# A wait of POOL in the middle of each group's eight gathers, in both layers of a two-layer graph network

## The chip, the cores and the metric

The kernel runs on one core of a Trainium2 chip. The metric is the device time of one execution in microseconds; the median of several runs is compared. Beside the timed runs there is one execution recorded by the hardware profiler, from which all rows here come.

## The reference, cut to what matters

There are 12,500 nodes with 128 features and 200,000 edges sorted by destination, `dst`, with random sources, `src`. Layer 0 is an attention layer over the edges, layer 1 sums the neighbours with edge features and puts two matrix products behind them. Both read one row of a node table for each edge, by `src`.

```python
# layer 0: loops added to the edges
xl = (x @ W_l).reshape(N, HEADS, C); xr = (x @ W_r).reshape(N, HEADS, C)
h = xl[src] + xr[dst]
e = jnp.einsum('ehc,hc->eh', leaky_relu(h, 0.2), att)
p = jnp.exp(e - segment_max(e, dst)[dst])
alpha = p / segment_sum(p, dst)[dst]
out = segment_sum(alpha[:, :, None] * xl[src], dst).reshape(N, HID) + bias + x
x = layernorm(x + layernorm(out) * gamma + beta)
# layer 1
neigh = segment_sum(x[src] + edge_attr_128, dst)
h = leaky_relu((2.0 * x + neigh) @ W1 + b1, 0.01)
x = layernorm(x + (h @ W2 + b2))
```

## The kernel before, in words

The work has three phases with a barrier of all engines behind the first and the second. In the first, `node_loop` makes the tables `xl_table` (528 bytes a node: the product and four linear terms) and `xr_table` from `x`. The second is layer 0, the third layer 1.

Both layers walk over 196 groups of 1024 edges (128 partitions, `T` = 8 edges each). Four sets of buffers (`U` = 4) go around: `src_idx`, `rows`, `dst_row` and others. Each engine has its own program, a loop over groups, and the engines meet by semaphores.

SP loads for each group the indices `src_idx` (4 KB, line 614 in layer 0, line 1416 in layer 1) and the larger pieces: in layer 0 the destinations of the group repeated on all partitions (`dst_row`, 513 KB, line 607) and a window of `xr_table`; in layer 1 the edge features (`dst_row` again, 512 KB, line 1419) and a window of `x1_table`. In layer 0 the indices of a group are loaded one group ahead (`AHEAD` = 1), in layer 1 three groups behind the group whose sum is done (`BACK` = 3).

POOL issues the gathers: for each group eight indirect DMAs of 128 rows each (line 671 from `xl_table`, line 1446 from `x1_table`), each with one index per partition. In layer 0 it waits for the indices and for the set of rows (`rows_free0`, signalled by DVE's line 1124 four groups before); in layer 1 for the indices alone, which are loaded only when the set is free. Each gather adds 16 to the set's own semaphore `gathered0` or `gathered1` when its data has landed.

PE waits for the whole group, 128 on that semaphore, before its first product of the rows (`sources`, line 694, and `sum_group`, line 1460). In layer 0 a step of PE is: `sources` of the next group, two transposes, `targets` (line 703), `sum_up` of the last group (line 745), `attend` (line 729), `pick_last` (line 767). ACT and DVE make the softmax between them; DVE's line 1112 waits for `attend`, ACT's line 925 for `sum_up`. In layer 1 PE sums features and rows into a bank and signals `neigh_summed`; DVE's line 1631 adds the bank to the nodes' sums, and PE's lines 1483 to 1496 make the two products of one window of nodes, a window a group.

`wait_alone` is a wait for a semaphore as an instruction of its own, followed by one that adds 1 to a count of waits.

Of the kernel before, what the change touches and what calls it, by code (L numbers as in the profile page):

```python
# [30 lines left out]
T = 8  # L31
# [116 lines left out]
def wait_alone(eng, waits, sem, value):  # L148


    eng.wait_ge(sem, value)
    eng.sem_inc(waits, 1)
# [20 lines left out]
def build(nc, a, out, edges, groups, blocks):  # L173
# [6 lines left out]
    with ctx:  # L180
# [81 lines left out]
        def by_head(t):  # L262
# [15 lines left out]
        pool_waits, pe_waits, v_waits, sp_waits, act_waits = (  # L278
            nc.alloc_semaphore(n) for n in ("pool_waits", "pe_waits", "v_waits", "sp_waits", "act_waits"))
        sems = {}  # L280

        def S(name):
            if name not in sems:
                sems[name] = nc.alloc_semaphore(name)
            return sems[name]
# [45 lines left out]
        with nc.Block() as block:  # L331
            @block.sync
            def _(sp):
                for t, n in ((w_lr[:, 0:D], "W_l"), (w_lr[:, DW:DW + D], "W_r")):
                    sp.dma_start(t, a[n]).then_inc(S("products_in"), 16)

                def load(q):
                    if q.at_least(2 * R):
                        sp.wait_ge(S("x_taken"), q.times(1, 1 - 2 * R))
                    s = q.c % (2 * R)  # L340
                    sp.dma_start(ring_x[s], x_pair[q.times(1)]).then_inc(S(f"x_in{s}"), 16)

                def store(q):
                    s = q.c % R
                    sp.wait_ge(S("xl_ready"), q.times(1, 1))
                    sp.dma_start(xl_pair[q.times(1)], ring_w[s]).then_inc(S(f"xl_out{s}"), 16)
                    sp.wait_ge(S("xr_ready"), q.times(1, 1))
                    sp.dma_start(xr_pairs[q.times(1)], xr_pair[:, q.times(1)]).then_inc(S("xr_out"), 16)

                node_loop(sp, pairs, [(load, 0), (store, 7)])  # L350
                for g in range(AHEAD):
                    sp.dma_start(src_idx[g][:, :], bass.AP(a["src"].tensor, g * G, [[T, P], [1, T]]))\
                      .then_inc(S(f"src_in0{g}"), 16)
                sp.wait_ge(S("xr_out"), 16 * pairs)
                for s in range(R):
                    sp.wait_ge(S(f"xl_out{s}"), 16 * (pairs // R))
# [260 lines left out]
        with nc.Block() as block:  # L617
# [45 lines left out]
            @block.gpsimd  # L663
            def _(pool):
                with pool.Fori(0, groups // U) as j:
                    for s in range(U):

                        wait_alone(pool, pool_waits, S(f"src_in0{s}"), j * 16 + 16)
                        wait_alone(pool, pool_waits, S(f"rows_free0{s}"), j + 1)
                        for t in range(T):  # L670
                            pool.indirect_dma_start(rows[s][:, t, :], None, xl_table[:, :],  # L671
                                                    bass.IndirectOffsetOnAxis(ap=src_idx[s][:, t:t + 1], axis=0))\
                                .then_inc(S(f"gathered0{s}"), 16)
# [729 lines left out]
        with nc.Block() as block:  # L1403
# [35 lines left out]
            @block.gpsimd  # L1439
            def _(pool):  # L1440
                with pool.Fori(0, groups // U) as j:
                    for s in range(U):

                        wait_alone(pool, pool_waits, S(f"src_in1{s}"), j * 16 + 16)
                        for t in range(T):
                            pool.indirect_dma_start(rows[s][:, t, 0:D], None, x1_table[:, :],  # L1446
                                                    bass.IndirectOffsetOnAxis(ap=src_idx[s][:, t:t + 1], axis=0))\
                                .then_inc(S(f"gathered1{s}"), 16)
# [284 lines left out]
```

## Time and profile before

| | us |
|---|---|
| median of 3 runs | 4110.53 |
| lowest and highest | 4109.94 and 4111.07 |
| profiled execution, span of its instructions | 5652.3 |
| of this busy: PE, POOL, DVE, ACT | 3416.6, 2973.6, 2121.7, 1585.3 |

The page gives no time for the profiled execution but its span; what lies around the first and the last instruction is not in it. The profiled execution is far longer than the timed ones. In rows of the timeline the columns are the start in us, the duration in us, engine, line, operation, what it writes and reads, how many instructions the row merges, and in brackets the idle time of the engine before it and what ended it. An engine name with a q behind it is its queue, where DMAs are issued.

### The profile page before, as it was taken

How to read it: one execution, taken by the hardware profiler on the slowest of the kernel's cores; microseconds unless marked ns; L12 is line 12 of the kernel's file. 1: busy time of each engine (PE TensorE's matmuls, PEld its weight loads, DVE VectorE, ACT ScalarE, POOL GpSimd, SP SyncE). 2: the span in 40 equal slices, each digit the busy share in tenths (PEclk: the TensorE clock that was granted, in tenths of full speed). 3: DMA queues.
4: the chain of work that ended last, by engine and by line, in shares of the span. 5: the costliest groups of instructions: out<-in, count | busy, mean ns of one | idle time of the engine just before them, and what ended most of it. 6: DMA issues, size and time to landing. Idle time of an engine off the chain costs nothing. (4 is left out here: it accounts for less than half of the span.)

```text
span 5652.3 us, 80469 instructions
## 1 busy us (share of the span) xinstructions
PE 3416.6 (60%) x19294; PEld 2795.9 (49%) x19295; DVE 2121.7 (38%) x8176; ACT 1585.3 (28%) x3447; POOL 2973.6 (53%) x3194
## 2 busy tenths in 40 slices
PE   5667676766666766767666455545555555555554
PEld 4455454545445544545544444445455455545454
DVE  4454554545544544545545122222222222222222
ACT  3343443334333433334333111111111111111111
POOL 2454454544554554555552656555555565555554
PEclk8787888778887878778877677777777777777777
DMA  7333333333333333333332533333333333333332
GB/s 227 81 97 89 91 94 86 93 82 92 92 88 86 94 87 86 90 85 95 91 88 59 102 91 93 92 90 93 92 92 93 92 93 92 93 91 93 92 93 70
DMA packets 459582, 525.88 MB, mean 93 GB/s; under 512 B 199115, under 2 KB 359287, under 8 KB 459551
## 3 DMA queue, kind: packets, MB, share of 16 engines
q1 hardware_dynamic: 266498, 268.35, 16.3%
q0 software_dynamic: 100352, 208.93, 15.3%
q10 hardware_dynamic: 92701, 48.23, 3.0%
q8 instruction: 13, 0.21, 0.0%
q14 instruction: 18, 0.15, 0.0%
HBM read 471.23 MB, written 53.95 MB: 93 GB/s over the span
## 5 line engine op out<-in xcount | busy, mean ns | idle before, releaser
L671 POOL DMA_INDIRECT rows<-xl_table,src_idx x1568 | 1482.2, 945 | 1458.0 <-DVE wmsg L1124 655.5
L1446 POOL DMA_INDIRECT rows<-x_table,src_idx x1568 | 1480.4, 944 | 1102.7 <-issue 605.8
L1491 PE MATMUL ph<-ident,relu_h 128*128 128x128 f32 x196 | 83.9, 428 | 1103.0 <-DVE relu_h L1636 726.0
L1491 PEld LDWEIGHTS ph<-ident,relu_h 128*128 128x128 f32 x196 | 33.0, 168 | 1164.0 <-DVE relu_h L1636 755.5
L703 PE MATMUL ph<-node_of,xr_win 128*128 128x512 f32 x784 | 517.8, 797 | 5.9 <-issue 5.1
L745 PE MATMUL pA<-wmsg,edge_of 128*128 128x136 f32 x3136 | 430.7, 293 | 94.9 <-issue 56.9
L911 ACT ACTIVATE relu_h<-ph 128x512 f32<-128x512 f32 x392 | 232.1, 597 | 849.3 <-PE ph L703 551.9
L1532 ACT ACTIVATE relu_h<-ph,b 128x128 f32<-128x128 f32 x196 | 72.0, 367 | 1383.6 <-PE ph L1496 1044.1
L745 PEld LDWEIGHTS pA<-wmsg,edge_of 128*128 128x128 f32 x3136 | 402.7, 199 | 104.8 <-issue 100.5
L767 PE MATMUL pA<-win,last_node 128*1 128x136 f32 x392 | 99.0, 345 | 573.7 <-ACT win L925 513.1
L729 PE MATMUL pT<-att_heads,relu_h 128*128 128x48 f32 x3136 | 383.6, 272 | 79.0 <-issue 52.5
L729 PEld LDWEIGHTS pT<-att_heads,relu_h 128*128 128x128 f32 x3136 | 375.6, 194 | 71.7 <-issue 39.4
L965 ACT ACTIVATE node_of<-dst_row,first_node 128x1024 f32<-128x1024 int32 x196 | 406.3, 2073 | 5.6 <-issue 4.9
L694 PE MATMUL ph<-ident,rows 128*128 128x128 f32 x1568 | 309.2, 362 | 57.8 <-issue 57.8
L1112 DVE TENSOR_TENSOR logits<-pT,rows 128x32 f32<-128x32 f32 x196 | 39.8, 203 | 752.8 <-remote 626.2
L767 PEld LDWEIGHTS pA<-win,last_node 128*1 128x1 f32 x392 | 20.8, 80 | 608.6 <-issue 605.7
L694 PEld LDWEIGHTS ph<-ident,rows 128*128 128x128 f32 x1568 | 253.1, 189 | 122.1 <-issue 117.4
L1460 PE MATMUL pT<-node_of,dst_row 128*128 128x128 f32 x1568 | 300.1, 372 | 0.0
L1460 PEld LDWEIGHTS pT<-node_of,dst_row 128*128 128x128 f32 x1568 | 296.3, 290 | 0.8
L1631 DVE TENSOR_TENSOR xr<-xr,pA 128x128 f32 x98 | 28.3, 288 | 707.9 <-DMA w_lr<-in_W_r 699.1
L703 PEld LDWEIGHTS ph<-node_of,xr_win 128*128 128x128 f32 x784 | 191.8, 271 | 192.3 <-issue 180.7
L1460 PE MATMUL pA<-edge_of,dst_row 128*128 128x128 f32 x1568 | 285.3, 359 | 0.8 <-issue 0.7
(174 smaller groups left out, 6322.4 us busy)
## 6 DMA issues: line engine op xcount, KB each, us to landing
dst_row<-in_dst SPq DMA_DIRECT2D x196, 513.0 KB
dst_row<-in_edge_attr SPq DMA_DIRECT2D x195, 512.0 KB
rows<-xl_table,src_idx POOLq DMA_INDIRECT x1568
rows<-x_table,src_idx POOLq DMA_INDIRECT x1568
sums_table<-win ACTq DMA_DIRECT2D x196, 68.0 KB
xr_win<-xr_table SPq DMA_DIRECT2D x196, 64.0 KB
relu_h<-x_table SPq DMA_DIRECT2D x196, 64.0 KB
out_x<-relu_h ACTq DMA_DIRECT2D x196, 64.0 KB
```

The source lines that it names most:

```text
L671: pool.indirect_dma_start(rows[s][:, t, :], None, xl_table[:, :], bass.IndirectOffsetOnAxis(ap=src_idx[s][:, t:t + 1], axis=0))\
L694: pe.matmul(h[:, t, :], rows[s][:, t, 0:D], ident[:, :], start=(t % 4 == 0), stop=False, is_transpose=True)
L703: return [pe.matmul(h[:, k:k + 4, :], xr_of[:, :], by_tile[:, k:k + 4, :], start=False, stop=stop) for k in range(0, T, 4)]
L729: ins = pe.matmul(out_t[:, t, :], relu_h[0][:, t, :], att_heads[:, :], start=(t == 0), stop=(t == T - 1))
L745: ins = pe.matmul(pA[k][:, 0:WC], edge_of[k][:, t, :], w[:, t, :], start=(t == 0), stop=(t == T - 1))
L767: pe.matmul(pick, last_node[:, g.c % U:g.c % U + 1], win[:, :], start=True, stop=True)\
L911: act.activation(relu_h[0][:, k:k + 4, :], h, ACT.Relu, scale=1.0 - GAT_SLOPE)\
L965: act.activation(in_tiles(node_of[g.c % 2][:, :]), ids, ACT.Abs, scale=-1.0, bias=first_node[:, s:s + 1])\
L1446: pool.indirect_dma_start(rows[s][:, t, 0:D], None, x1_table[:, :], bass.IndirectOffsetOnAxis(ap=src_idx[s][:, t:t + 1], axis=0))\
L1460: ins = pe.matmul(bank, m[:, t, :], one_hot[:, t, :], start=(k == 0 and t == 0), stop=(k == 1 and t == T - 1))
L1491: pe.transpose(across_bank, x1_slot[s], ident[:, :]).then_inc(S("x1_across"), 1)
L1532: act.activation(of, z_bank, ACT.Identity, bias=b1[:, 0:1])
```

## The change

Between the fourth and the fifth gather of each group, in both layers, POOL waits until its semaphore says that the first four gathers of this group have landed (64 above what the earlier rounds of this set left, 128 for each).

```diff
                         wait_alone(pool, pool_waits, S(f"src_in0{s}"), j * 16 + 16)
                         wait_alone(pool, pool_waits, S(f"rows_free0{s}"), j + 1)
                         for t in range(T):
+                            if t == T // 2:
+                                wait_alone(pool, pool_waits, S(f"gathered0{s}"), j * (16 * T) + 16 * (T // 2))
                             pool.indirect_dma_start(rows[s][:, t, :], None, xl_table[:, :],
                                                     bass.IndirectOffsetOnAxis(ap=src_idx[s][:, t:t + 1], axis=0))\
                                 .then_inc(S(f"gathered0{s}"), 16)
...
                         wait_alone(pool, pool_waits, S(f"src_in1{s}"), j * 16 + 16)
                         for t in range(T):
+                            if t == T // 2:
+                                wait_alone(pool, pool_waits, S(f"gathered1{s}"), j * (16 * T) + 16 * (T // 2))
                             pool.indirect_dma_start(rows[s][:, t, 0:D], None, x1_table[:, :],
                                                     bass.IndirectOffsetOnAxis(ap=src_idx[s][:, t:t + 1], axis=0))\
                                 .then_inc(S(f"gathered1{s}"), 16)
```

## Rows read from the trace of the kernel before

**Rows 1.** The page: span, and busy time of each engine.
```profile
span 5652.3 us, 80469 instructions
...
PE 3416.6 (60%) x19294; PEld 2795.9 (49%) x19295; DVE 2121.7 (38%) x8176; ACT 1585.3 (28%) x3447; POOL 2973.6 (53%) x3194
```

**Rows 2.** Table of stretches: layer 0, between, layer 1, end; clock and DMA last.
```profile
104.90:3034.09 2929.19, 1987.22 (x10757) 1458.70 (x10757) 1453.23 (x6061) 1130.60 (x2359) 1482.18 (x1568) 0.80 0.35 92
3034.09:3109.34 75.25, 41.69 (x191) 31.02 (x190) 36.61 (x155) 18.36 (x55) 0.01 (x1) 0.74 0.12 28
3109.34:5617.16 2507.82, 1296.33 (x7899) 1238.21 (x7899) 556.41 (x1728) 381.49 (x862) 1480.37 (x1568) 0.76 0.34 93
5617.16:5652.30 35.14, 19.11 (x137) 18.14 (x137) 9.70 (x37) 6.15 (x18) 0.00 (x0) 0.79 0.06 14
```

**Rows 3.** Timeline of POOL, two groups of layer 0 behind each other, first and last.
```profile
1609.69 0.94 POOL L671 DMA_INDIRECT rows<-xl_table,src_idx  x1 [0.30 <-issue]
1610.94 0.94 POOL L671 DMA_INDIRECT rows<-xl_table,src_idx  x1 [0.30 <-issue]
...
1627.16 0.94 POOL L671 DMA_INDIRECT rows<-xl_table,src_idx  x1 [0.30 <-issue]
```

**Rows 4.** What POOL waited for, whole span: us in total, times, longest.
```profile
POOL rows L671 <- DVE wmsg L1124: 655.5, 61, 16.9
...
POOL rows L1446 <- DMA src_idx<-in_src: 496.8, 109, 6.8
...
POOL rows L671 <- DMA src_idx<-in_src: 319.4, 85, 4.6
```

**Rows 5.** What DVE and ACT waited for in layer 0, whole span.
```profile
DVE logits L1112 <- remote: 626.2, 62, 16.6
```
```profile
ACT win L925 <- remote: 699.7, 129, 16.6
```

**Rows 6.** Timeline of all engines around a standstill in layer 0.
```profile
1617.23 1.89 PE L729 MATMUL pT<-att_heads,relu_h 128*128 128x48 f32 x16
...
1631.05 0.28 ACT L925 ACTIVATE win<-pA 128x136 f32<-128x136 f32 x1 [14.12 <-remote]
1631.14 0.21 DVE L1112 TENSOR_TENSOR logits<-pT,rows 128x32 f32<-128x32 f32 x1 [12.77 <-remote]
...
1631.48 0.61 PE L767 MATMUL pA<-win,last_node 128*1 128x136 f32 x2 [12.37 <-ACT win L925]
```

**Rows 7.** Timeline of DVE behind the last gather of layer 1.
```profile
5628.67 0.29 DVE L1631 TENSOR_TENSOR xr<-xr,pA 128x128 f32 x1 [3.83 <-PE pA L1460]
...
5634.80 0.29 DVE L1631 TENSOR_TENSOR xr<-xr,pT 128x128 f32 x1 [0.17 <-PE pT L1460]
...
5641.02 0.29 DVE L1631 TENSOR_TENSOR xr<-xr,pT 128x128 f32 x1 [2.32 <-PE pT L1460]
```

**Rows 8.** Timeline, layer 1: SP's load of indices and the gather it releases, twice.
```profile
4004.03 0.33 SPq L1416 DMA_DIRECT2D src_idx<-in_src  x1
...
4006.48 0.94 POOL L1446 DMA_INDIRECT rows<-x_table,src_idx  x1 [4.25 <-DMA src_idx<-in_src]
...
4029.51 0.33 SPq L1416 DMA_DIRECT2D src_idx<-in_src  x1
...
4031.82 0.94 POOL L1446 DMA_INDIRECT rows<-x_table,src_idx  x1 [4.63 <-DMA src_idx<-in_src]
```

**Rows 9.** DMA: the gathers' queue, and loads with median us to landing last.
```profile
q0 software_dynamic: 100352, 208.93, 15.3%
...
sums<-xl_table SPq DMA_DIRECT2D x51, 132.0 KB, 2.3
...
sums<-in_x SPq DMA_DIRECT2D x51, 128.0 KB, 2.5
...
rows<-in_x SPq DMA_DIRECT2D x50, 128.0 KB, 2.1
```

**Rows 10.** Timeline: last gather of the first group, first product that reads its rows.
```profile
113.79 0.94 POOL L671 DMA_INDIRECT rows<-xl_table,src_idx  x1 [0.30 <-issue]
...
120.25 1.94 PE L694 MATMUL ph<-ident,rows 128*128 128x128 f32 x8 [9.22 <-issue]
```

## The prediction

> **What bounds the kernel now.** I read the page first, then the table of stretches, then POOL's own rows, and last the places where the whole core stands still.
>
> The page shows no engine that is full: PE is busy 60% of a span of 5652.3 us, POOL 53% [rows 1]. The span itself is the first thing to explain: the runs have a median of 4110.53 us, so the profiled execution is 5652.3 - 4110.5 = 1541.8 us (38%) longer than the runs that are timed. Whatever fills those 1541.8 us is in the profile and not in the time, and a reading of the waits at face value would be a reading of something else.
>
> The stretches split the span at POOL's first and last gather of each layer [rows 2]: 104.9 us of node work ahead, 2929.19 us for layer 0 (196 groups, 14.9 us each), 75.25 us between, 2507.82 us for layer 1 (12.8 us each), 35.14 us at the end. The three parts without gathers come to 104.9 + 75.25 + 35.14 = 215.3 us.
>
> POOL does nothing in the layers but issue gathers, eight to a group, 1568 to a layer. Each is 0.94 us busy with 0.30 us before the next [rows 3]: a start every 1.2475 us or so (1609.69 to 1627.16 is 14 steps, 1.248 each). The reader is to see that this run crosses a border of groups without a wider step: a wait on POOL that is already satisfied costs nothing that shows. So POOL alone needs 8 x 1.248 = 9.98 us for a group, 392 x 9.98 = 3913 us for all, and with the 215.3 us around it 4128 us. The median of the runs is 4110.5, 0.4% below that. I read this as: in the timed runs POOL issues gathers back to back all the time, and its issue rate is what the kernel takes.
>
> The check from the other side: in the profile POOL stands idle beyond its own steps for 2929.2 + 2507.8 - 3913 = 1524 us, and 1541.8 us is what the profiled execution is longer. Nearly all of its waits for freed buffers (655.5 us) and for indices (319.4 and 496.8 us) [rows 4] are then in the profile alone. What makes them is seen in the chain of waits and the timeline. DVE and ACT wait 626.2 and 699.7 us for something the profile calls remote in layer 0 [rows 5]. In one such place PE starts its last product at 1617.23 for 1.89 us, and nothing on ACT, DVE or PE starts until ACT does at 1631.05, DVE at 1631.14, PE at 1631.48 [rows 6]: signals of PE that should be there at 1619.1 act 12 us later. After the last gather the same loop takes 6.2 us a group: DVE's addition starts right behind PE's end at 5628.67, 5634.80 and 5641.02 [rows 7]. The other engines of layer 1 thus need about 6.2 us a group where POOL needs 9.98. In layer 0 PE is busy 1987.22/196 = 10.1 us a group at a granted clock of 0.80, that is between 8.1 us (all at full clock) and 10.1, so close behind POOL.
>
> **The change, part by part.** It removes nothing and moves nothing: per group one wait and one semaphore increment on POOL, between the fourth and the fifth gather, 392 in all. The gathers, their number and their order stay. The increment and a wait that is satisfied show no cost at the borders of groups [rows 3]: I take 0. Queued behind the wait on POOL are the group's gathers five to eight and all later groups' gathers; PE waits for all eight of a group. No DMA of SP or ACT is moved or passed, since they are other queues.
>
> The wait is not satisfied when POOL comes to it. It asks for the landing of a gather that POOL has just issued, so POOL idles from the end of the fourth gather until its rows are in SBUF and the semaphore says so. That gap takes the place of the 0.30 us that stand there now. No row shows a gather awaited by POOL, so I bound the gap.
>
> Nearest rows from below: a 4 KB index load is issued by SP at 4004.03 (0.33 us) and POOL's waiting gather starts at 4006.48; the next pair is 4029.51 and 4031.82 [rows 8]: 2.3 to 2.45 us from the start of the issue to POOL's start. Plain loads of 128 to 132 KB land 2.1 to 2.5 us after issue [rows 9], so for 64 KB the size hardly counts. If these times ran from the start of the gather instruction, whose descriptors are written while it is busy, 2.3 - 0.94 = 1.4 us would be left as the gap; if from its end, 2.3 to 2.5 us. Nearest row from above: the first group's last gather starts at 113.79 and ends at 114.73; PE's first product that reads the rows starts at 120.25 [rows 10], 5.5 us later, while ACT's 6.9 MB of zeros (the page's largest single issue) were being written. That is a landing under load. In the layers DMA is a third busy [rows 2], and the gathers' queue moves a gather's data in 0.153 x 5652.3/3136 = 0.28 us of each engine [rows 9], so a single collision with another transfer adds tenths, not microseconds. I take 2.3 us, nearer to the small loads: the last descriptors of a gather are ready only at its end, which pulls to the upper case, and the early ones are already under way, which pulls to the lower.
>
> The sum: 2.3 - 0.30 = 2.0 us a group, 2.0 x 392 = 784 us. None of it is covered: the cover would be POOL's idle time, and the timed runs have none. Against the profile's own parts that is 4128 + 784 = 4912; against the median, which I use, 4110.5 + 784 = 4895 us. The new period is 12.0 us; PE needs 8.1 to 10.1 in layer 0 and 6.2 in layer 1, so POOL stays the bound. Later starts of later gathers also mean later indices and free buffers, but those are asked for a ring of three or four groups ahead, and POOL being slower makes them earlier by comparison.
>
> The Trainium skill, in "DMA: Bandwidth & Descriptors", section "Anatomy of one DMA — SWDGE (gpsimd) path", gives about 2.0 us plus bytes/436e3 for one such DMA, nearly all of it the confirmation that the data has landed. By it a gather of 64 KB takes 2.15 us as an estimate; laid behind the gather's end that would give (2.15 - 0.30) x 392 = 725 us and 4836 us, laid from its start 357 us and 4468 us. The plain loads of [rows 9] agree with it, and no row here shows a gather's.
>
> **The rivals.**
>
> Absorbed (no change). Taken at face value the profile has POOL idle 1524 us at borders of groups, 3.9 us a group, more than the 2.0 us added; a wait in the middle would only take the place of the one at the border, and the time would stay 4110. For it: those waits are large and real in the profile [rows 4]. Against it: they would have to be in the timed runs too, and 4110.5 has no room for them beside 3913 us of issuing. It decides if the step between gathers is shorter in timed runs.
>
> Partly absorbed. If the 0.30 us between gathers come with profiling, the step is 0.94 us, POOL needs 7.5 us a group and has 2.4 us of slack in the (4110.5 - 215.3)/392 = 9.94 us of a group. Then POOL's period is 8 x 0.94 + 2.3 = 9.8 us, nothing is added, and we are at the case above; halfway, with a step of 1.1 us, it is 8.8 - 0.16 + 2.3 = 10.9 us against 9.94, 392 x 1.0 = 390 us, and 4500 us. Against it: the fit of 4128 to 4110 would be chance.
>
> Longer landing, or a cold PE. With a gap of 3.5 us (a 513 KB row of node numbers or a 512 KB block of edge features in the way every group) it is 3.2 x 392 = 1254 us and 5365 us. A PE that idles 4 us of 12 and falls to the lower clock in layer 0 would need up to 10.1 x 0.80/0.50 = 16.2 us a group there if all of it ran at 1.2 GHz. Against that: in the profile, at 14.9 us a group and so with more idle time, the mean granted was 0.80 and the work 10.1 us [rows 2], under the 12.0 us of the new period. I give it only the same upper end.
>
> Faster. The late signals of PE [rows 6] hold all engines while POOL issues without a pause, and at 1631.05 they come 2.95 us after POOL's last gather ended (1628.1). If a stream of gathers holds them back, a pause in mid-group lets them through, and PE, ACT and DVE run sooner. In the profile that is worth up to 626 us in layer 0. It pays only if those stalls, not POOL, set the timed 9.94 us a group, and if POOL with its pause still needs less: with a step of s that is 7s + 0.94 + 2.3 < 9.94, so s under 0.96 us, where the profile has 1.248 and the busy time alone is 0.944. At 0.944 it would be 9.85 us a group, 392 x 0.09 = 35 us and 4075 us.
>
> **How the numbers follow.** Full price with a gap of 1.9 to 2.9 us (4740 to 5130 us): 0.62. Gap of 1.4 to 1.9, or partly absorbed (4500 to 4740): 0.17. Longer landing or cold PE (5130 to 5400 and beyond): 0.14. Absorbed: 0.05. Faster: 0.02. The predicted time is that of the first, 4895 us. The range must hold 0.8: all of the first, most of the second and half of the third, 4550 to 5250 us. A measurement of this kernel, whose three runs span 0.03%, tells a change from none at about 0.2%; slower by more than that are the first three cases, 0.93, within it 0.05, faster 0.02.
>
> **What the profile of the changed kernel would show.** The fifth gather of each group preceded by idle time of about 2.3 us, ended by a DMA, 392 times, where 0.30 us stand now; the busy time of a gather still 0.94 us and 1.25 us between the others. POOL's waits for freed buffers and indices shrink, since in the profile (not in the time) they are there to be replaced; so the profiled span grows by less than the timed 784 us. If the gap were near 1.4 or 3.5 us, the size is wrong and the step is right. If the gap is 2.3 us and the time still 4110, then the reading of POOL as the bound is wrong, and with it the whole.

## The result, and the profile after

The changed kernel takes 5063.02 us (median of 4 runs, 5053.62 to 5066.17) beside 4110.8 us (4109.94 to 4112.89) for the kernel before: a ratio of 1.2315, 95% interval 1.23 to 1.2329. The forecast was 4895 us, range 4550 to 5250. It is 952 us slower, 2.43 us for each of 392 groups; forecast were 784 us and 2.0 us.

The kernel before has two times: medians of 4110 to 4117 us on some chips (the first kind below) and of 5660 to 5670 us on others (the second kind); every comparison below was made on one chip, and the profile of before [rows 1, 2] is, by its span, of the second kind, that of after of the first.

The page of the changed kernel, the lines that answer to [rows 1], and below them those of its slices for PE's clock:

```profile
span 5061.6 us, 80959 instructions
...
PE 3402.5 (67%) x19294; PEld 2808.9 (55%) x19295; DVE 2115.3 (42%) x8176; ACT 1582.5 (31%) x3447; POOL 2975.7 (59%) x3194
...
PEclk9888888888888888888887777777777777777777
```

The span is within 2 us of the run's own time of 5063.47. The busy times are within 1% of those of before: nothing was added to do. The table of stretches, cut as in [rows 2] at POOL's first and last gather of a layer:

```profile
106.40:2610.10 2503.70, 1904.68 (x10814) 1409.89 (x10812) 1472.04 (x6112) 1136.00 (x2381) 1484.48 (x1568) 0.86 0.42 108
2610.10:2671.60 61.50, 28.84 (x134) 22.29 (x134) 24.74 (x103) 9.83 (x33) 0.12 (x1) 0.75 0.06 17
2671.60:5041.40 2369.80, 1387.60 (x7990) 1318.94 (x7990) 550.04 (x1752) 385.35 (x873) 1479.92 (x1568) 0.78 0.36 98
5041.40:5061.60 20.20, 8.04 (x46) 7.42 (x46) 2.71 (x13) 2.69 (x8) 0.08 (x1) 0.73 0.06 15
```

Layer 0 takes 12.8 us a group, layer 1 12.1 us. What POOL waited for, beside [rows 4]:

```profile
POOL rows L673 <- DMA rows<-xl_table,src_idx: 601.4, 196, 7.3
POOL rows L1450 <- issue: 479.2, 1372, 61.4
POOL rows L1450 <- DMA rows<-x_table,src_idx: 472.1, 196, 5.8
POOL rows L673 <- issue: 429.3, 1372, 11.5
```

The waits for freed rows and for indices are gone. In their place stand 196 waits in each layer for POOL's own gathers: 601.4/196 = 3.07 us in layer 0, 472.1/196 = 2.41 us in layer 1. The other 1372 gathers of each layer have their 0.30 us of "issue" as before. Their sum less the 0.30 us that stood there before is 601.4 + 472.1 - 392 x 0.30 = 956 us, beside the 952 us timed. The timeline of POOL at two pauses, one in each layer; the number in brackets is the idle time:

```profile
1603.04 0.95 POOL L673 DMA_INDIRECT rows<-xl_table,src_idx  x1 [0.30 <-issue]
1604.29 0.94 POOL L673 DMA_INDIRECT rows<-xl_table,src_idx  x1 [0.30 <-issue]
1609.44 0.94 POOL L673 DMA_INDIRECT rows<-xl_table,src_idx  x1 [4.21 <-DMA rows<-xl_table,src_idx]
...
4008.74 0.94 POOL L1450 DMA_INDIRECT rows<-x_table,src_idx  x1 [0.30 <-issue]
4012.06 0.94 POOL L1450 DMA_INDIRECT rows<-x_table,src_idx  x1 [2.38 <-DMA rows<-x_table,src_idx]
```

Layer 1 is regular (2.31 to 2.49 us in a row of nine pauses). Layer 0 goes up and down: of twelve pauses behind each other, seven took 2.33 to 2.44 us and five 3.29 to 4.48 us. SP's queue at the long one above shows a large load close by, the 513 KB of destination numbers, issued while the fourth gather was being made (1604.29 to 1605.23):

```profile
1604.41 0.33 SPq L605 DMA_DIRECT2D dst_near<-in_dst  x1
...
1604.84 0.38 SPq L607 DMA_DIRECT2D dst_row<-in_dst  x1
```

Whether a pause is long goes by the time of that load. In the timelines from 400 to 2400 us there are 156 pauses. In 65 the load was issued before the fourth gather ended, and they took 3.85 us on average (2.82 to 4.58); in 91 it was issued later, and they took 2.43 us (2.30 to 2.83), as in layer 1.

Who waits for the pause is seen from PE: before its first product of a group's rows it now stands 535.0 us in layer 0 and 727.1 us (366.2 + 360.9) in layer 1, each time for a gather.

```profile
PE ph L696 <- DMA rows<-xl_table,src_idx: 535.0, 191, 15.7
PE pT L1464 <- DMA rows<-x_table,src_idx: 366.2, 98, 4.5
PE pA L1464 <- DMA rows<-x_table,src_idx: 360.9, 97, 4.6
```

### The profile page after: what moved, and what is told of

Same layout as the page of the kernel before. It is cut to its first block and busy times, and to the rows that moved or that the text cites. A ratio compares the mean times of both kernels' runs of the same rounds, so it can differ in the third digit from the quotient of the medians.

```text
span 5061.6 us, 80959 instructions
## 1 busy us (share of the span) xinstructions
PE 3402.5 (67%) x19294; PEld 2808.9 (55%) x19295; DVE 2115.3 (42%) x8176; ACT 1582.5 (31%) x3447; POOL 2975.7 (59%) x3194
## 3 DMA queue, kind: packets, MB, share of 16 engines
q1 hardware_dynamic: 266498, 268.35, 17.9%
## 5 line engine op out<-in xcount | busy, mean ns | idle before, releaser
L673 POOL DMA_INDIRECT rows<-xl_table,src_idx x1568 | 1484.6, 947 | 1030.7 <-DMA rows<-xl_table,src_idx 601.4
L696 PE MATMUL ph<-ident,rows 128*128 128x128 f32 x1568 | 299.6, 354 | 535.2 <-DMA rows<-xl_table,src_idx 535.0
L1464 PE MATMUL pT<-node_of,dst_row 128*128 128x128 f32 x1568 | 354.7, 418 | 366.2 <-DMA rows<-x_table,src_idx 366.2
L1464 PE MATMUL pA<-edge_of,dst_row 128*128 128x128 f32 x1568 | 355.2, 419 | 361.4 <-DMA rows<-x_table,src_idx 360.9
L1464 PEld LDWEIGHTS pT<-node_of,dst_row 128*128 128x128 f32 x1568 | 331.0, 321 | 382.0 <-issue 382.0
L1464 PEld LDWEIGHTS pA<-edge_of,dst_row 128*128 128x128 f32 x1568 | 331.8, 322 | 377.3 <-issue 377.3
L705 PE MATMUL ph<-node_of,xr_win 128*128 128x512 f32 x784 | 537.4, 825 | 0.0
L747 PE MATMUL pA<-wmsg,edge_of 128*128 128x136 f32 x3136 | 409.7, 284 | 68.9 <-DVE edge_of L1159 68.7
L747 PEld LDWEIGHTS pA<-wmsg,edge_of 128*128 128x128 f32 x3136 | 381.7, 190 | 77.5 <-issue 73.5
L1159 DVE TENSOR_TENSOR edge_of<-dst_rel,pT 128x1024 f32<-128x1024 f32 x196 | 239.3, 1221 | 96.8 <-DVE dst_rel L1156 91.4
L1635 DVE TENSOR_TENSOR xr<-xr,pT 128x128 f32 x98 | 28.3, 288 | 541.8 <-PE pT L1464 541.8
L1146 DVE COPY carry_f<-carry_f 4x1 f32<-4x1 f32 x196 | 27.7, 142 | 538.7 <-PE pT L812 538.4
```

What stands on the lines that cost most here:

```text
L696: pe.matmul(h[:, t, :], rows[s][:, t, 0:D], ident[:, :], start=(t % 4 == 0), stop=False, is_transpose=True)
L705: return [pe.matmul(h[:, k:k + 4, :], xr_of[:, :], by_tile[:, k:k + 4, :], start=False, stop=stop) for k in range(0, T, 4)]
L747: ins = pe.matmul(pA[k][:, 0:WC], edge_of[k][:, t, :], w[:, t, :], start=(t == 0), stop=(t == T - 1))
L1159: one_hot = lambda k: v.tensor_tensor(edge_of[k][:, :, :], dst_rel[:, :].unsqueeze(2).to_broadcast([P, T, P]), near_row.unsqueeze(1).to_br ...
L1464: ins = pe.matmul(bank, m[:, t, :], one_hot[:, t, :], start=(k == 0 and t == 0), stop=(k == 1 and t == T - 1))
```

## The experiments

**1. A wait that is already satisfied.** In both layers, in the place of the wait of the change (layer 0 is shown):

```diff
-    wait_alone(pool, pool_waits, S(f"gathered0{s}"), j * (16 * T) + 16 * (T // 2))
+    wait_alone(pool, pool_waits, S(f"src_in0{s}"), j * 16 + 16)
```

> The wait stands in the same place, in both layers, but asks for what POOL has already waited for (the indices of the group), so it never waits. My theory, that only the landing costs: 4110 us within 0.2%, since a satisfied wait shows no wider step at the borders of groups. Rival, that a further semaphore wait and its increment break up POOL's stream of gathers by themselves: some of the 952 us stay; at 0.2 us each it would be 392 x 0.2 = 78 us and 4190 us.

5654.57 us (10 runs) beside 5660.09 us (19 runs), ratio 0.9994, 0.9964 to 1.0023. The chip was one of the second kind, which I had not expected: there POOL has idle time at the borders of groups, and a small price could hide in it. It shows only that the instruction costs nothing that is seen there. Where POOL is the bound this kernel was not timed; experiments 7 and 10 have satisfied waits there, and show what these cost.

**2 and 3. Waiting for older gathers.** The first k gathers (k = 3, 2) signal a semaphore of their own, and POOL waits for these. The edit for k = 3 in layer 0, cut; layer 1 has the same:

```diff
+    wait_alone(pool, pool_waits, S(f"early0{s}"), j * 48 + 48)
...
-    .then_inc(S(f"gathered0{s}"), 16)
+    .then_inc(S(f"early0{s}" if t < 3 else f"gathered0{s}"), 16)
...
-    wait_alone(pe, pe_waits, S(f"gathered0{s}"), g.use(16 * T, 16 * T))
+    wait_alone(pe, pe_waits, S(f"early0{s}"), g.use(48, 48))
+    wait_alone(pe, pe_waits, S(f"gathered0{s}"), g.use(80, 80))
```

> The first three gathers of a group signal a semaphore of their own, and POOL waits in the middle for these three, not for four; PE waits for both semaphores. The oldest awaited gather is then one step of 1.248 us further on. Mean gap of the change 3.07 us in layer 0 and 2.41 in layer 1; less 1.248: 1.82 and 1.16, less the 0.30 that stand there anyway: 1.52 and 0.86 us, 196 x 2.38 = 467 us, so 4577 us. Rival, that a pause costs by itself whatever it waits for (restarting the queue of gathers): over 4800 us.

> As the kernel that waits for three, but for the first two gathers. Gaps of 3.07 - 2.50 = 0.57 and 2.41 - 2.50 under zero: in layer 0 only the groups whose landing is late wait, in layer 1 none. By theory about 0.4 us for a group of layer 0 on average, 196 x 0.4 = 78 us, and 4110 to 4200 us. Rival, a price of a pause by itself: over 4400 us.

On the same chip as experiment 1, beside 5660.09: 5665.79 us for two (ratio 1.002, 0.999 to 1.005). For three there is no such interval: three of four runs took 5646 to 5667 us, within the 5637 to 5690 of before, and one took 5452 us, at a granted clock of 0.60 where the others had 0.78; why is not known. No cost is seen of either. The profile with the wait for three shows why. What POOL waited for:

```profile
POOL rows L673 <- DVE wmsg L1127: 754.3, 93, 13.2
...
POOL rows L1451 <- DMA src_idx<-in_src: 360.8, 90, 6.4
POOL rows L673 <- DMA rows<-xl_table,src_idx: 184.6, 129, 5.6
POOL rows L1451 <- DMA rows<-x_table,src_idx: 174.9, 148, 4.5
...
POOL rows L673 <- DMA src_idx<-in_src: 32.8, 14, 3.8
```

POOL waits 359.5 us in the middle of groups, and less at the borders: 754.3 + 360.8 + 32.8 = 1147.9 us where [rows 4] has 1471.7. This is what the rival "absorbed" of the prediction describes, on a chip where POOL's issuing alone is not the bound.

**4. Seven gathers in place of eight**, the kernel before otherwise (`range(T - 1)` around the gathers, 112 in place of 128 for PE).

> The kernel before with seven gathers a group in place of eight; the eighth eighth of the rows is never read from the tables (in layer 0 it is zero, in layer 1 what was there), all other work stays. If POOL's issuing is what the timed runs take, 392 x 1.248 = 489 us less: 3621 us, or a little more where PE's work in layer 0 (8.1 to 10.1 us a group against 8.73) begins to bound. Rival, that something else sets the 9.94 us a group and the fit with 8 x 1.248 is chance: about 4110 us.

5092.18 us beside 5660.09 us, ratio 0.9008 (0.8965 to 0.9052): 568 us less. This is on the chip of experiments 1 to 3, so it does not test the bound of the 4110 us. It says that there, too, the time hangs on the gathers, by 1.45 us for each of 392, more than the 1.248 us that POOL takes to issue one.

**5. The changed kernel again.**

> The changed kernel again, on the chip of these comparisons, where the kernel before took 5660 us (19 runs) and not the 4110.8 us that it took when the change was timed. The profile of before, 5652.3 us with its standstills, then shows a real way for this program to run, not an effect of profiling. Theory: a pause for the landing of all gathers in flight ends the standstills; then the changed kernel takes its own 5063 us here too, and is faster than before by 10%. Rival: this chip is slower for whatever kernel; then 5063 x 5660/4110.8 = 6970 us.

5070.72 us beside 4112.17 us, ratio 1.2322 (1.23 to 1.2345). The chip was one of the first kind again. The result repeats; neither side of what was expected for the second kind was tested, and whether the pause helps there was not measured.

**6 and 7. One layer alone.** The wait in layer 0 only, and in layer 1 only.

> The pause in layer 0 alone. If the pause sets a layer's time by itself: layer 0 with its 2504 us as in the changed kernel, layer 1 with the 2508 us that it has in the profile of before on a chip like this (the changed kernel has 2370), so some 5200 us beside 5660; where the kernel before takes 4110.8 us it would be 4110.8 + 196 x (3.07 - 0.30) = 4654 us. Rival, a slower chip for all: about 6300 us.

> The pause in layer 1 alone. With layer 0 as in the profile of before (2929 us) and layer 1 as in the changed kernel (2370 us): some 5515 us beside 5660; where the kernel before takes 4110.8 us, 4110.8 + 196 x (2.41 - 0.30) = 4524 us. Rival, a slower chip for all: about 6200 us.

4656.02 us (ratio 1.1326, 1.1307 to 1.1345) and 4521.82 us (1.0997, 1.0978 to 1.1015) beside 4112.17 us, against 4654 and 4524 worked out for such a chip. The two prices, 544 and 410 us, add up to 954 us; both pauses cost 959 us on this chip (experiment 5). The kernel with the pause in layer 1 alone is also the best look at the kernel before in its 4110 us: its layer 0 is untouched. What POOL waited for there:

```profile
POOL rows L671 <- issue: 463.1, 1483, 11.5
...
POOL rows L671 <- DMA src_idx<-in_src: 14.0, 46, 0.3
POOL rows L671 <- DVE wmsg L1124: 11.9, 39, 0.3
```

All of these average 0.31 us or less, the first one of 11.5 us aside: POOL issues all 1568 gathers back to back. In experiment 6 it is layer 1 that is untouched, and there it is the same:

```profile
POOL rows L1448 <- issue: 541.7, 1567, 64.4
```
```profile
L1448 POOL DMA_INDIRECT rows<-x_table,src_idx x1568: 938/944/2192, 2658.5 to 4615.8; - x196
```

This last row is from the list of the line's instructions, its last times being the first and the last start: 1957.3 us apart, 1.249 us for each of 1567 steps. For layer 0 in experiment 7 it is 1960.6 us, 1.251 us a step:

```profile
L671 POOL DMA_INDIRECT rows<-xl_table,src_idx x1568: 940/945/1197, 106.1 to 2066.7; - x196
```

The place of [rows 6] looks like this in that layer 0:

```profile
1004.73 1.88 PE L729 MATMUL pT<-att_heads,relu_h 128*128 128x48 f32 x16
1005.00 0.28 ACT L925 ACTIVATE win<-pA 128x136 f32<-128x136 f32 x1 [0.47 <-PE pA L736]
...
1006.65 0.20 DVE L1112 TENSOR_TENSOR logits<-pT,rows 128x32 f32<-128x32 f32 x1 [0.71 <-PE pT L729]
```

ACT starts 0.11 us behind the product of PE that it waits for (line 736, which ends at 1004.89) and DVE 0.04 us behind the end of `attend` at 1006.61, where in [rows 6] 12 us pass. PE's clock there, the table of stretches for 400 to 2000 us:

```profile
400.00:2000.00 1600.00, 1391.45 (x8902) 1059.25 (x8902) 1202.05 (x5049) 952.96 (x1966) 1210.26 (x1279) 0.98 0.51 135
```

PE is busy 87% of the time at a granted clock of 0.98, nearly all at the 2.4 GHz level: 0.87 x 10.0 = 8.7 us a group. It has 1.3 us to spare, so POOL is the bound with PE close behind. The same work took 10.1 us at 0.80 in [rows 2].

**8. Three pauses a group**, at `t in (2, 4, 6)`, each for all that are in flight.

> Three pauses a group in place of one: behind the second, the fourth and the sixth gather, each for all that are in flight. If each costs its landing less 0.30 us: 4110.8 + 3 x 952 = 6967 us, on any chip, since POOL is then far the slowest. Rival, that later pauses find less in flight and cost less: under 6300 us.

6960.01 us, ratio 1.6937 (1.6906 to 1.6967), 7 us from the sum. Three times the pauses cost three times the price:

```profile
POOL rows L673 <- DMA rows<-xl_table,src_idx: 1713.3, 588, 6.9
POOL rows L1450 <- DMA rows<-x_table,src_idx: 1481.4, 588, 6.2
```

**9 and 10. Waiting for three and for two, again.**

> The wait for the first three gathers once more, since its first comparison ran on a chip where the kernel before took 5660 us and POOL's idle time at the borders of groups covered the pause. Where the kernel before takes 4111 us: 4577 us as worked out before (gaps of 1.82 and 1.16 us in place of 0.30). Rival, a price of the pause by itself: over 4800 us. Should this chip be one where before takes 5660 us, both expect about 5650 us again.

> The wait for the first two gathers once more, for the same reason. Where the kernel before takes 4111 us: 4110 to 4200 us, since 2.41 us of landing are less than the two steps of 1.248 us that are issued meanwhile, and only late landings of layer 0 show. Rival, a price of the pause by itself: over 4400 us.

Now beside 4116.96 us: 4457.15 us for three (1.0824, 1.0806 to 1.0842) and 4169.26 us for two (1.0125, 1.0108 to 1.0141). Two is in its range. Three is 120 us below 4577. The layer 1 part is near what was worked out (221.8/196 = 1.13 us for 1.16); in layer 0 the gap is 235.0/196 = 1.20 us and not 1.82. First the kernel that waits for three, then the one for two:

```profile
POOL rows L673 <- DMA rows<-xl_table,src_idx: 235.0, 196, 6.2
POOL rows L1451 <- DMA rows<-x_table,src_idx: 221.8, 196, 4.4
```
```profile
POOL rows L673 <- issue: 473.4, 1517, 10.7
POOL rows L1451 <- DMA rows<-x_table,src_idx: 81.4, 128, 3.0
...
POOL rows L673 <- DMA rows<-xl_table,src_idx: 22.8, 51, 3.1
```

For two, the time was as expected and the split was not: the late landings were to be in layer 0 and none in layer 1, and POOL waited 51 times in layer 0 and 128 times in layer 1. It is again a matter of when a large load is issued: in 57 of the last 192 groups of layer 1 SP had issued the 512 KB of edge features 0.75 to 2 us before the end of the second gather, and POOL stood 1.04 us on average; in the 135 others it stood 0.31 us. The other 213 waits were satisfied when POOL came to them, and stand at the 0.30 us of any step (in layer 0, (473.4 - 10.7)/1516 = 0.31 us): a satisfied wait in the middle of a group costs nothing that shows where POOL is the bound.

In a timeline of nine pauses of layer 0, eight took 1.06 to 1.11 us and one 1.42 us. The long landings of the changed kernel are not there, though SP issues its load at the same point of POOL's step as before (0.4 to 1.8 us behind the start of the fourth gather; in the changed kernel 0.4 to 2.3). What differs is the gather that is awaited: of 157 pauses from 400 to 2100 us none had the load issued before the third gather had been over for 0.68 us, and none took longer than 1.47 us. A row without a collision gives the landing of a gather by itself: from the end of the third gather to the start of the fifth it is 0.30 + 0.94 + 1.08 = 2.32 us, and without an older gather in between 2.3 to 2.45 us.

**11. The changed kernel with less traffic in layer 0.** The edit, cut; `dst_row` is also set to zero once at the start of the layer:

```diff
-    sp.dma_start(dst_row[s][:, 0:G + 2], bass.AP(a["dst"].tensor, g.times(G), [[0, P], [1, G + 2]]))
+    parts = P if g.j is None else 16
+    sp.dma_start(dst_row[s][0:parts, 0:G + 2], bass.AP(a["dst"].tensor, g.times(G), [[0, parts], [1, G + 2]]))
```

> The changed kernel, with the 513 KB load of destination numbers in layer 0 cut to 16 of the 128 partitions from the second group on (the other partitions keep zeros, so sources and destinations are matched wrongly; all instructions stay). My theory is that this load is what makes layer 0's landing 3.07 us where layer 1's is 2.41: the gap falls to 2.4 us, 196 x 0.66 = 129 us less than the changed kernel, about 4935 us. Rival, that the rest of layer 0's traffic (windows, sums, merges) or its rows of 528 bytes are what makes it longer: about 5063 us.

4979.59 us, 83 us under the changed kernel's 5063 (timed on another chip of the first kind) where 129 were expected. The pauses of layer 0 fall to 520.0/196 = 2.65 us:

```profile
POOL rows L674 <- DMA rows<-xl_table,src_idx: 520.0, 196, 6.8
...
POOL rows L1452 <- DMA rows<-x_table,src_idx: 460.7, 196, 5.8
```

So seven eighths of the load of destination numbers make (601.4 - 520.0)/196 = 0.42 of the 0.66 us by which layer 0's landing is longer. The rest goes by the same moment: of 162 pauses from 400 to 2400 us, 87 had the thinned load issued before the end of the fourth gather and took 2.82 us on average, 75 had it later and took 2.36 us. SP issues three loads there within about 1 us, `dst_near`, `dst_row` and the window of `xr_table`; which of them makes the rest was not separated. That rows of 528 bytes land later by themselves, the rival of this experiment, has nothing left to explain: without such a load in the way layer 0 lands as layer 1 does (2.36 and 460.7/196 = 2.35 us).

**12. Seven gathers, again.**

> Seven gathers a group in place of eight once more, without a wait (an eighth of the rows is never read from the tables), since its first comparison ran where the kernel before took 5660 us. Where before takes 4111 us and POOL's issuing is the bound: 392 x 1.248 = 489 us less, 3622 us. POOL's period would be 8.74 us; PE in layer 0 needs 8.1 us at full clock, so 0 to 80 us more if it just begins to bound. Rival, that another loop sets the 9.94 us a group: over 3900 us. Should this chip be one where before takes 5660 us: 5092 us again.

5109.71 us beside 5670.18 us, ratio 0.9023 (0.8962 to 0.9083). The chip was, once more, one of the second kind, and the result repeats experiment 4. That seven gathers would take 3622 us on the first kind was thus not seen; that POOL is the bound there rests on experiments 6 to 10.

All comparisons on chips of the first kind, against one sum: the time of before beside them, plus the idle time ended by a gather in the profile, less 0.30 us for each such pause.

| kernel | pauses | idle, us | sum, us | measured, us |
|---|---|---|---|---|
| change | 392 | 1073.5 | 5067 | 5063 |
| change, again | 392 | 1076.5 | 5071 | 5071 |
| layer 0 alone | 196 | 587.2 | 4641 | 4656 |
| layer 1 alone | 196 | 468.6 | 4522 | 4522 |
| three pauses | 1176 | 3194.7 | 6954 | 6960 |
| for three | 392 | 456.8 | 4456 | 4457 |
| for two | 179 | 104.2 | 4168 | 4169 |
| change, thin load | 392 | 980.7 | 4980 | 4980 |

(The profile of layer 0 alone is of a run of 4639.6 us.)

## Why the prediction was right, point by point

The bound: right for the runs that were timed. The argument from arithmetic (3136 gathers at 1.248 us plus 215.3 us make 4128) is confirmed by experiments 6 and 7, whose untouched layers issue without a gap, and by the table: a microsecond of pause is a microsecond of time. The fit within 17 us had some luck in it. The 215.3 us come from a profile of the second kind and are 27 us too much: the parts without gathers in the changed kernel's stretches are 106.4 + 61.5 + 20.2 = 188.1 us. The steps are a little longer than 1.248 us, 1.251 in layer 0 and 1.249 in layer 1 (experiments 7 and 6); with these it is 3920 + 188 = 4108 us.

The reason given for the profile's 1541.8 us more was wrong in one point. I wrote that the waits are "in the profile alone", and expected the profiled span to grow by less than the time. It shrank from 5652.3 to 5061.6 us, the time of the run itself. The 5652.3 us are not an effect of profiling but another way in which the kernel before runs: 5660 and 5670 us in timed runs on two other chips, with the same standstills (DVE's and ACT's waits for something remote are 628.9 and 707.1 us in the profile of experiment 1, beside 626.2 and 699.7 in [rows 5]). The rival "absorbed" is what happens there with smaller pauses (experiments 2 and 3). It had the right mechanism for the wrong chips. That the change was timed on a chip of the first kind was luck, as far as the prediction goes: I did not know that there were two kinds, and on the second the arithmetic of the bound does not hold.

The price of the wait itself: 0, as taken; the satisfied waits at the borders in experiment 7, and those in the middle of groups in experiment 10, stand at 0.30 us like any other step.

The gap: the term of 2.3 us was mis-sized. It is 2.41 us in layer 1, where 2.3 to 2.5 had been read off plain loads laid behind the gather's end [rows 8, 9]; the lower bound of 1.4 us, counted from the gather's start, is ruled out. In layer 0 it is 3.07 us. There my step was that a collision "adds tenths, not microseconds". It went by the 0.28 us that a gather's own 64 KB take, and what stands in the way is a load of eight times the size. By the queue that SP's loads go through in the changed kernel's profile (packets, MB, share of the time of 16 engines), 513 KB take 0.179 x 5061.6 x 0.525/268.35 = 1.8 us of each engine, as an estimate:

```profile
q1 hardware_dynamic: 266498, 268.35, 17.9%
```

Single collisions added up to 2.2 us between 400 and 2400 us; over all pauses of layer 0 it is 0.66 us on average, more than half of it from this load (experiment 11). The two corrections are 196 x 0.11 + 196 x 0.77 = 172 us, and 4895 + 172 = 5067 us.

The Trainium skill's fit in "DMA: Bandwidth & Descriptors", section "Anatomy of one DMA — SWDGE (gpsimd) path", gave 2.15 us for such a gather as an estimate. Laid behind the instruction's end it is near the 2.3 to 2.45 us of an undisturbed pause, somewhat low; laid from its start it is not borne out, since from there such a gather takes 0.94 + 2.3 to 2.45 = 3.2 to 3.4 us.

Longer landing or a cold PE: the first came in part, in layer 0. The second did not: PE was granted 0.86 in layer 0, was busy 1904.68/196 = 9.7 us of 12.8, and waited for gathers 191 times.

Faster by letting PE's late signals through: no run here shows it. The changed kernel has no such standstill, but on the chips where it was run the kernel before has none either.

## What to carry to other kernels

A wait for the landing of a DMA that the same engine has just issued costs the whole landing, here 2.4 us undisturbed and 3.1 us on average among other traffic, against 0.30 us between two issues; waiting for one that is two issues older cost 0.13 us a group (52 us for 392). How long the landing takes depends on what is issued just before: look where other queues' large loads fall in relation to the awaited transfer, and wait for one that has landed before they start. When the span of a profile and the timed median are far apart (here 38%), add up the engine's own issue times and see which of the two they leave room for, and do not put the rest down to profiling before another chip has been timed.

## What the runs showed of the hardware that I had not expected

The same program ran in 4109 to 4118 us or in 5623 to 5690 us, by chip: of the four chips of the experiments two were of the first kind (7 runs each), two of the second (19 and 7 runs), never both on one. Each chip was used at one time only, so whether it is the chip or something else about that moment cannot be told. The mean granted clock is 0.89 in the first and 0.78 in the second; that the clock is the cause is unlikely, since the one run of experiment 2 at 0.60 was the shortest there, 5452 us.

On the second kind PE's signals come late, by 12 us in the place of [rows 6]; no profile of the first kind, all of kernels with a pause in at least one layer, has a single wait for something remote. In the profile of before, between 400 and 2800 us, DVE waits 37 times for more than 6 us for such a signal. In 27 of these it starts 2.7 to 3.2 us after the end of POOL's last gather, in 25 of the 27 behind a run of 15 or 16 gathers without a pause; in six others it starts while gathers are being issued. One gather a group less saves 560 to 568 us there (experiments 4 and 12). Both point to the stream of gathers as part of the cause. It cannot be all of it: on the first kind the stream goes on for 1568 gathers (experiments 6 and 7), and nothing is late. What it is, and whether the pause of this change would shorten the 5660 us, stays open.
